# Second experts: each slot tile's weights fetched by SyncE into a ring, against weights resident in SBUF and addressed by register

## The reference

```python
logits = x_flat @ Wr + br
probs = jax.nn.softmax(logits, axis=-1)
topk_w, topk_idx = jax.lax.top_k(probs, 2)              # of 16 experts
topk_w = topk_w / jnp.clip(jnp.sum(topk_w, axis=-1, keepdims=True), 1e-09)
h = jnp.einsum('nc,ech->neh', x_flat, W1) + b1
h = jax.nn.gelu(_layernorm(h, g1, be1), approximate=False)
expert_out = jnp.einsum('neh,eho->neo', h, W2) + b2
sel = jnp.take_along_axis(expert_out, topk_idx[:, :, None], axis=1)
y_flat = jnp.sum(sel * topk_w[:, :, None], axis=1)
```

## Time and profile before

| | before |
|---|---|
| median of 3 runs | 3978.86 us (3962.93 to 3979.88) |
| profiled execution | 3980.16 us, its span 3977.9 |
| mean granted TensorE clock | 0.877 |
| busy share of the span: TensorE, VectorE, ScalarE, GpSimd | 70%, 61%, 40%, 47% |
| second experts | 3439.8 (first load) to about 3787 us of the span |
| two attentions | 2323 to about 3190 us |

### The profile page before, as it was taken

One profiled execution on the slowest core, in us unless ns is written; L12 is line 12 of the kernel. 1 busy time (PEld: TensorE's weight loads), 2 busy tenths in 40 slices (PEclk: granted clock), 3 DMA queues, 4 the chain that ended last, 5 costly groups with the idle time before them and its releaser, 6 DMA issues.

```text
span 3977.9 us, 93960 instructions
## 1 busy us (share of the span) xinstructions
PE 2801.2 (70%) x28526; PEld 1944.6 (49%) x28529; DVE 2445.7 (61%) x6828; ACT 1588.0 (40%) x3994; POOL 1863.6 (47%) x2306
## 2 busy tenths in 40 slices
PE   3999999758888888882058879999999930266600
PEld 2666666435555555551036656666666620255500
DVE  2777777528878878884001148888888860155545
ACT  2666666424545545541013335555555510011100
POOL 4222222006766666663730036666666617411177
PEclk9999999978989989985579989999999965699955
DMA  2111111351111111111222211111111102211133
GB/s 52 42 41 39 39 41 44 117 172 42 50 47 49 48 48 49 47 32 34 77 71 74 67 39 30 30 28 30 29 30 30 26 11 78 64 55 55 54 85 87
DMA packets 282379, 207.17 MB, mean 52 GB/s; under 512 B 61731, under 2 KB 246456, under 8 KB 281905
## 3 DMA queue, kind: packets, MB, share of 16 engines
q1 hardware_dynamic: 262960, 164.88, 14.1%
q0 software_dynamic: 19200, 39.62, 3.7%
HBM read 114.99 MB, written 90.18 MB: 52 GB/s over the span
## 4 chain that ended last, share of the span: by engine, by line
issue 21%; PE 14%; POOL 13%; DVE 5%; POOLq 0%; ACT 0%; DMA 0%; DVEq 0%; ACTq 0%; SPq 0%
PE scores_ps L1049 3%; POOL k_bd L2001 2%; POOL rows L2053 2%; POOL shared L2152 2%; POOL shared L2001 2%; POOL got L2098 2%; PE heads_ps L1056 1%; PE desk_ps L1056 1%; PE scores_ps L1167 1%; POOL norm_rstd L1997 1%; PE scores_ps L1169 1%; PE heads_ps L1167 1%; DVE e_T L1821 1%; PE desk_ps L1167 1%; POOL rstd L2160 1%
## 5 line engine op out<-in xcount | busy, mean ns | idle before, releaser
L1997 POOL TENSOR_TENSOR norm_rstd<-norm_veps,minus_half 128x1 f32<-128x1 f32 x384 | 218.3, 569 | 380.6 <-DVE norm_veps L1557 374.8
L2053 POOL DMA_INDIRECT rows<-e_in,slot_put x256 | 248.9, 972 | 164.0 <-issue 107.4
L1278 ACT ACTIVATE probs<-probs 128x512 f32<-128x512 f32 x384 | 239.9, 625 | 107.6 <-DVE probs L1577 107.2
L1575 DVE TENSOR_REDUCE row_max<-scores_ps 128x8 f32<-128x512 f32 x384 | 261.9, 682 | 26.0 <-issue 16.1
L1577 DVE TENSOR_TENSOR probs<-scores_ps,row_max 128x512 f32<-128x512 f32 x384 | 265.4, 691 | 13.2
L1282 ACT ACTIVATE turned<-scores_ps 128x512 f32<-128x512 f32 x384 | 228.1, 594 | 109.2 <-PE scores_ps L907 103.5
L907 PE MATMUL scores_ps<-consts,probs 128*128 128x128 f32 x1536 | 243.1, 282 | 7.3 <-ACT probs L1278 6.5
L1210 ACT ACTIVATE probs<-probs 128x512 f32<-128x512 f32 x256 | 161.4, 630 | 141.4 <-DVE probs L1496 138.5
L1494 DVE TENSOR_REDUCE row_max<-scores_ps 128x8 f32<-128x512 f32 x256 | 174.7, 682 | 57.0 <-PE scores_ps L763 57.0
L2142 POOL TENSOR_TENSOR o_rstd<-o_veps,minus_half 128x2 f32<-128x2 f32 x72 | 49.9, 693 | 288.7 <-DVE o_veps L1926 288.7
L907 PEld LDWEIGHTS scores_ps<-consts,probs 128*128 128x128 f32 x1536 | 176.2, 143 | 16.0 <-ACT probs L1278 9.8
(11 more groups left out here) (335 smaller groups left out, 8327.6 us busy)
## 6 DMA issues: line engine op xcount, KB each, us to landing
hop_dram<-shared SPq DMA_DIRECT2D x64, 256.0 KB, 2.1
hop_in<-hop_dram SPq DMA_DIRECT2D x64, 256.0 KB, 3.0
rows<-zero_rows SPq DMA_DIRECT2D x64, 144.0 KB, 1.9
shared<-rows SPq DMA_DIRECT2D x72, 128.0 KB, 2.1
moe<-shared SPq DMA_DIRECT2D x72, 128.0 KB, 1.8
rows<-zero_rows SPq DMA_DIRECT2D x64, 128.0 KB, 1.8
c_in<-in_ctx SPq DMA_DIRECT2D x128, 64.0 KB, 1.9
c_two<-in_ctx SPq DMA_DIRECT2D x128, 64.0 KB, 2.4
```

What stands on the lines that cost most here:

```text
L1278: act.activation(half, half, ACT.Exp, scale=scale).then_inc(at.exped.sem, 1)
L1575: dve.tensor_reduce(best, sc, AX, ALU.max).then_inc(at.shift.sem, 1)
L1997: pool.tensor_tensor(n_rstd[:, k, u, :], n_veps[:, k, u, :], minus_half[:, 0:1], ALU.pow).then_inc(sig.sem, 1)
L2053: pool.indirect_dma_start(out=rows, out_offset=bass.IndirectOffsetOnAxis(ap=slot_put[:, c, U * n + i:U * n + i + 1], axis=0), in_=put_rows ...
```

## The change

The second mixture's weights no longer stay in SBUF. At the start of the third stage they are written to a packed table in DRAM, `e_dram`: 128 rows of 258 numbers per expert, W1, W2, scale and shift side by side. In the sixth stage SyncE reads the pair's two expert numbers and copies two experts' 128 x 258 numbers (132 KB each) into a ring of four places, `fetched`, one place a pair; a place is written when the second layer of the pair four before is done. TensorE and ScalarE take weights, scale and shift from the place at fixed addresses, and wait for its two transfers. The biases lie in 16 rows, `bias_rows`; the bias matmul now has as its stationary input a one-hot column of the expert (`chosen`), which GpSimd copies for each pair out of a table, `expert_row`, that one new VectorE instruction in the second routing makes. In `combine5` the copy is gone: the two multiply-adds read their weights from the table by a register, and the counts of `norms[0]` fall from 7 to 6 a tile. GpSimd also clears `bias_rows` at the start, for which SyncE's first waits count one more.

```diff
--- before.py
+++ after.py
@@ -172,8 +172,9 @@
         hop_rows = sb("hop_rows", [P, HOPS, D])
         hop_T = sb("hop_T", [P, HOPS, P])
-        o_w1, o_w2 = hop_rows[:, 0:E1, :], hop_rows[:, E1:2 * E1, :]
-        o_b1, o_b2 = hop_T[:, 0:E1, :], hop_T[:, E1:2 * E1, :]
+        EW = 2 * P + 2
+        fetched, chosen = sb("fetched", [P, V, 2, EW]), sb("chosen", [P, V, 2])
+        bias_rows = sb("bias_rows", [P, 2 * P])
...
+        e_dram = dram("e_dram", [E1 * P, EW])
+        e_rows = e_dram.rearrange("(e p) n -> e p n", p=P)
...
@@ -438,11 +440,10 @@
-            (o_w1, T["L1_ffn_W1"].rearrange("e c h -> c e h")),
-            (o_w2, T["L1_ffn_W2"].rearrange("e c h -> c e h")),
-            (o_b1.rearrange("p e h -> p (e h)"), T["L1_ffn_b1"].rearrange("e h -> (e h)").partition_broadcast(P)),
-            (o_b2.rearrange("p e h -> p (e h)"), T["L1_ffn_b2"].rearrange("e h -> (e h)").partition_broadcast(P)),
-            (o_g[:], T["L1_ffn_g1"].rearrange("e h -> h e")), (o_b[:], T["L1_ffn_be1"].rearrange("e h -> h e")),
+            (e_rows[:, :, 0:P], T["L1_ffn_W1"]), (e_rows[:, :, P:2 * P], T["L1_ffn_W2"]),
+            (e_rows[:, :, 2 * P:2 * P + 1], T["L1_ffn_g1"].rearrange("e (h o) -> e h o", o=1)),
+            (e_rows[:, :, 2 * P + 1:EW], T["L1_ffn_be1"].rearrange("e (h o) -> e h o", o=1)),
+            (bias_rows[0:E1, 0:P], T["L1_ffn_b1"]), (bias_rows[0:E1, P:2 * P], T["L1_ffn_b2"]),
...
+            def fetch(q, k):
+                experts = [sp.value_load(expert_of[0:1, bass.ds(2 * q + i, 1)], min_val=0, max_val=E1 - 1) for i in range(2)]
+                after(sp, (s["o_down"], q - 1))
+                for i, e in enumerate(experts):
+                    sp.dma_start(fetched[:, k, i, :], e_rows[bass.ds(e, 1)].rearrange("e p n -> p (e n)"))\
+                      .then_inc(e_fetched[k], 16)
+
+            sp.wait_ge(late, 16 * len(late_loads))
+            sp.wait_ge(routed, 2)
+
             def period(i, j, live_pair):
                 w = j % 2
                 if live_pair(i + 3):
                     load6(i + 3, 1 - w)
+                    fetch(i + 3, (j + 3) % V)
                 if live_pair(i - 2):
                     store6(i - 2, w)
...
-            def layer(q, w, bank, src, weights, biases, waits, done):
-
-                experts = experts_of(q)
-                after(pe, *waits)
-                for i, e in enumerate(experts):
-                    pe.matmul(bank[:, cols(i)], const("row0"), biases[:, bass.ds(e, 1), :].rearrange("p e h -> p (e h)"),
+            def layer(n, q, k, bank, src, waits, done):
+
+                after(pe, (e_chosen, q + 1), (e_fetched[k], 8 * (q - k) + 32), *waits)
+                part = slice(P * n, P * n + P)
+                for i in range(2):
+                    pe.matmul(bank[:, cols(i)], chosen[:, k, i:i + 1].broadcast_to([P, P]), bias_rows[:, part],
                               start=True, stop=False, skip_group_check=True)
-                    last = pe.matmul(bank[:, cols(i)], src[:, cols(i)],
-                                     weights[:, bass.ds(e, 1), :].rearrange("p e h -> p (e h)"),
+                    last = pe.matmul(bank[:, cols(i)], src[:, cols(i)], fetched[:, k, i, part],
                                      start=False, stop=True, skip_group_check=True)
                 last.then_inc(done, 1)
...
@@ -1432,13 +1440,11 @@
-                    experts = [act.value_load(expert_of[0:1, bass.ds(2 * i + k, 1)], min_val=0, max_val=E1 - 1)
-                               for k in range(2)]
-                    after(act, (s["o_down"], i + 1), (s["o_hturned"], i + 3))
-                    for k, e in enumerate(experts):
+                    after(act, (e_fetched[j], 8 * (i - j) + 32), (s["o_down"], i + 1), (s["o_hturned"], i + 3))
+                    for k in range(2):
                         cols = slice(P * k, P * k + P)
                         last = act.activation(o_g_T[w][:, cols], scores_ps[:, w, 1, cols], ACT.Gelu,
-                                              scale=o_g[:, bass.ds(e, 1)], bias=o_b[:, bass.ds(e, 1)])
+                                              scale=fetched[:, j, k, 2 * P:2 * P + 1], bias=fetched[:, j, k, 2 * P + 1:EW])
...
+                    link(dve.tensor_scalar(expert_row[:], r_ej[:], float(E - 1), const("lane"), ALU.min, ALU.is_equal))
...
             def combine5(n, u):
-                dve.tensor_copy(got_w[u], weight[:, :, bass.ds(n, 1)].rearrange("p k t -> p (k t)")).then_inc(norms[0].sem, 1)
-                after(dve, norms[0].of(n, 1), (in_loaded[u], X4_LOADS + 8 * (n - u) + 16), (got_loaded[u], 16 * (n - u) + 32))
-                dve.scalar_tensor_tensor(part_sum[u], got[u][:, 0:D], got_w[u][:, 0:1], x_in[u], ALU.mult, ALU.add)\
+                after(dve, (in_loaded[u], X4_LOADS + 8 * (n - u) + 16), (got_loaded[u], 16 * (n - u) + 32))
+                dve.scalar_tensor_tensor(part_sum[u], got[u][:, 0:D], weight[:, 0, bass.ds(n, 1)], x_in[u], ALU.mult, ALU.add)\
                    .then_inc(norms[0].sem, 1)
-                after(dve, norms[0].of(n, 2))
-                dve.scalar_tensor_tensor(x4_raw[u], got[u][:, D:2 * D], got_w[u][:, 1:2], part_sum[u], ALU.mult, ALU.add)\
+                after(dve, norms[0].of(n, 1))
+                dve.scalar_tensor_tensor(x4_raw[u], got[u][:, D:2 * D], weight[:, 1, bass.ds(n, 1)], part_sum[u], ALU.mult, ALU.add)\
                    .then_inc(norms[0].sem, 1)
...
+                if live_pair(i + 2):
+                    after(pool, (s["o_down"], i + 1))
+                    pool.tensor_copy(chosen[:, (j + 2) % V, :], expert_row[:, bass.ds(2 * (i + 2), 2)]).then_inc(e_chosen, 1)
                 if live_pair(i + 1):
                     pool.wait_ge(s["o_veps_done"], i + 4)
```

More of the change, by code:

```diff
@@ L83, in constants @@
     f["head8q"] = f["head4"] * MD ** -0.5
-    f["row0"] = (p[:, None] == 0) & (p[None, :] >= 0)
+    f["lane"] = p[:, None]
     b = {"tri16": p[:, None] <= p[None, :], "ones16": np.ones((P, P)), "ident16": np.eye(P), "causal16": np.where(t[None, :] <= (p % S)[:, None], 0.0, NEG)}
@@ L224, in build @@
         assert NJ % (2 * V) == 0
-        expert_of = sb("expert_of", [P, NJ], I32)
+        expert_of, expert_row = sb("expert_of", [P, NJ], I32), sb("expert_row", [P, NJ])
         slot_f, weight = sb("slot_f", [P, 2, NT]), sb("weight", [P, 2, NT])
@@ L261, in build @@
         logits1 = sb("logits1", [P, NT, E1])
-        o_g, o_b = sb("o_g", [P, E1]), sb("o_b", [P, E1])
         o_in, o_in_T, o_hn, o_g_T, o_out = (views(U * 2 * P * k, 2 * P) for k in range(5))
@@ L310, in build @@
         o_in_loaded, o_stored = ([sem(f"{k}{u}") for u in range(U)] for k in ("o_in_loaded", "o_stored"))
+        e_fetched, e_chosen = [sem(f"expert_weights_fetched{k}") for k in range(V)], sem("expert_chosen")
         z_loaded, z_stored = hx_loaded, x_stored
@@ L389, in build @@
         o_copied = [Signal(pad_copied, NT), Signal(oT_copied, NT)]
-        norms = [again(mixed, 7), again(m_shift, 4), again(f_norm, 4)]
+        norms = [again(mixed, 6), again(m_shift, 4), again(f_norm, 4)]
         norm_rstd = [again(m_rstd), again(f_rstd), again(r4_added)]
@@ L515, in _ @@
                 load1(n, n)
-            sp.wait_ge(zero_sem, 1)
+            sp.wait_ge(zero_sem, 2)
             def clear(n):
@@ L650, in load_x4 @@
             def load_x4(n, u):
-                after(sp, norms[0].of(n - 2, 2))
+                after(sp, norms[0].of(n - 2, 1))
                 sp.dma_start(x_in[u], tile_rows(r4_dram, n)).then_inc(in_loaded[u], 16)
@@ L1148, in _ @@
             pe.wait_ge(counts_read, 2)
-            def experts_of(q):
-                return [pe.value_load(expert_of[0:1, bass.ds(2 * q + i, 1)], min_val=0, max_val=E1 - 1) for i in range(2)]
             def cols(i):
@@ L1176, in period @@
                 if live_pair(i + 1):
-                    layer(i + 1, 1 - w, scores_ps[:, 1 - w, 0, :], o_in_T[1 - w], o_w1, o_b1,
+                    layer(0, i + 1, (j + 1) % V, scores_ps[:, 1 - w, 0, :], o_in_T[1 - w],
                           ((s["o_T_done"], i + 4), (s["o_hn_done"], i + 2)), s["o_up"])
@@ L1186, in period @@
                 if live_pair(i - 1):
-                    layer(i - 1, 1 - w, (heads_ps, desk_ps)[1 - w], o_g_T[1 - w], o_w2, o_b2,
+                    layer(1, i - 1, (j - 1) % V, (heads_ps, desk_ps)[1 - w], o_g_T[1 - w],
                           ((s["o_g_done"], i + 2), (s["o_out_done"], i)), s["o_down"])
@@ L1867, in period @@
                     combine5(i + 3, 1 - u)
-                    stats5(norms[0], 3, 0, i + 3, 1 - u, x4_raw[1 - u])
+                    stats5(norms[0], 2, 0, i + 3, 1 - u, x4_raw[1 - u])
                 if live(i):
@@ L1954, in _ @@
             pool.memset(zero_rows[:], 0.0).then_inc(zero_sem, 1)
+            pool.memset(bias_rows[:], 0.0).then_inc(zero_sem, 1)
             pool.memset(slot_get[:], 0)
@@ L2092, in get5 @@
             def get5(n, u):
-                after(pool, norms[0].of(n - 2, 3))
```

(1 more changed line is left out.)

## The result

The changed kernel took 3906.1 us in the median (four runs, 3896.88 to 3922.08), the kernel before 3979.24 in the runs beside it: a ratio of 0.9842, 95% interval 0.9818 to 0.9866. That is 1.6% faster, 73 us, and 4 us from the forecast. The execution that was profiled is the slowest of the four: 3922.08 us, its span 3919.9 and so 58 us shorter than the one of before. What is known of the 16 us by which it stands above its median is told at the end.

What follows compares the result with a forecast made beforehand. No engine bounds the whole; the second experts are bound by TensorE's register reads, in series with a chain through the engines. Terms: -61 + 2 - 8 - 3 = -70 us from the profiled 3980.16, giving 3910 us, range 3880 to 3935.

Steps and rivals of the forecast that it cites:

- SyncE becomes the bound: Second experts: SyncE's serial list of load, two reads, two fetches and store sets the period, 3.7 us a pair.
- 3.0 as TensorE's floor: Second experts: TensorE's own work, 216 / 72 = 3.0 us a pair, as the least period.
- two to three pairs ahead: Second experts: a fetch goes out 7 to 11 us before its use and lands in 2 to 3 us.
- The saving of 61 us: Second experts: period from 4.62 to 3.7 us, 0.92 us saved a pair, times 66 pairs.
- The combination, 8 us: Attentions: without the weight copy, the multiply-add takes over its wait for GpSimd; 8 us saved, between 0 and 33.
- The weights' load: Start of third stage: two 1 MB broadcasts dropped, packing into DRAM added; -3 us taken, between -9 and +7.
- the bytes do leave: Start of third stage: half of the load's bytes dropped, pieces as many as before; a reason for taking -3 us.
- The bound of +7: Start of third stage: if the small pieces cost twice as much, 7.4 us more.
- (1): Second experts: SyncE keeps up and TensorE's 3.0 us bounds; saving 107 us, total 3865; chance 0.16.
- (2): Second experts: SyncE's reads cost 0.56 us, not 0.28; period 4.26, saving 24 us, total 3947; chance 0.13.
- (3): Second experts: a computed-address fetch costs its issuer 1.4 us; period 5.3, 46 us slower, total 4017; chance 0.04.
- (4): Second experts: fetch not ahead, TensorE waits for each landing, one wait replaces another; about 3970; chance 0.05.

Runs made afterwards that it cites:

- the split run: Changed kernel with store on ScalarE's queue, table's loads moved to the first scatter, ScalarE also reading the second expert number and issuing its fetch: 3822.61 us (0.9613).

## Why the prediction was right, point by point

- **SyncE becomes the bound: right.** Forecast 3.7 us a pair, measured 3.86. Taking the store out of its list took 0.67 us off the period, reading the numbers twice put 1.08 on, and moving half of the list away uncovered the next bound at 2.99. The prediction had 3.0 as TensorE's floor, and that agreement is luck: the floor was the busy time of before divided by 72, but in the split run the same matmuls are busy for 2.54 us a pair, and the bound is the round through TensorE and VectorE. One step on the way was wrong too: that a fetch is "two to three pairs ahead" and its wait "met early in the steady part". In the change the first layer starts 2.3 us after its second fetch is issued (median), 63 of the 72 first layers wait for their fetch, and the lead of the ring is used up by SyncE's lateness. That TensorE's register reads were the bound before is read from the earlier trace rows and from the "issue" that went away; no run took the reads alone out.
- **The saving of 61 us: the number right, its parts not.** The period of before was mis-sized: the prediction took a pair of the transposes' records for missing, but all 144 are in the trace, so the 305 us hold 65 pairs and not 66, 4.69 us and not 4.62; the loads' own row gives 4.70. With 3.86 for 3.7 the loop saved 63 x (4.70 - 3.86) = 53 us, and not 61. The rest came where no term stood: at the end, from the loop's last load to the last store's issue, 26.4 us before (3758.1 to 3784.5) became 15.8 (3710.6 to 3726.4). Those are 11 us; a likely reason is that the last pairs have hardly any reads and fetches left to wait for. The start cost 2.3 more (22.1 to 24.4 us from the first load to the loop), forecast 2. That the sum of it is 61 again is luck.

```profile
L688 SPq DMA_DIRECT2D moe<-shared x72: 372/390/397, 3456.3 to 3784.5; - x72
```

- **The combination, 8 us: right, 9 measured**, and by the mechanism: the multiply-add takes 1.85 us in the median, the wait passed on. The Trainium skill, "SBUF — State Buffer", section "Who interferes with whom", has it that a VectorE instruction with two SBUF inputs contends with a GpSimd one that reads SBUF, that a copy can, and that on this chip a reduction never does. The traces agree: 1.85 us for the multiply-add, 1.73 for the copy, 0.146 for the reduction. The saving per tile was overrated, 0.17 us and not 0.3 (2.43 us from the end of the instruction in front to the end of the second multiply-add, against 2.26); 0.10 of the difference is the register step between the two multiply-adds. TensorE's gap before the transpose fell by 5.6 us in 52 tiles, 6.9 in 64; what the other 2 us are isn't shown.
- **The weights' load: wrong.** Forecast -3 us, measured +4.2. The step that failed is "the bytes do leave", as a reason for a gain. 2 MB did leave, and SyncE stands no shorter: 6.41 and 4.86 us in the columns and 3.75 in the small biases, where the last column alone took 7.42 before. Taking the small pieces away gave 5.8 us, and taking all six loads away 17.7; so the wait goes with the transfers that stayed, small pieces and matrices, and not with the bytes that left. The bound of +7 held.
- **Rivals.** (1) SyncE doesn't keep up; (2) its reads take 0.27 us, and the 600 ns of the Trainium skill, "DMA: Bandwidth & Descriptors", section "Latency and other measured facts", are not what this trace shows; (3) a fetch costs 0.35 us, not 1.4; (4) TensorE does wait for fetches, but for late ones: before the first layer the wait is 55.9 us in the change, 26.7 with the store moved, 77.3 with the reads doubled and 2.8 in the split, so it follows the length of SyncE's list and isn't the way round the ring.
- **The sum.** -61 - 9 + 4 = -66 by the three stages, where -70 was forecast; the medians say -73, the profiled executions -58. Of the 8 us between -66 and -58, 4.5 are the third stage (876.8 us before and 881.3 after from the first to the last load of `hop_in`), and 2.8 lie between the combination's last load and the first pair's, 297.9 and 300.7 us; in the other runs with the same routing this takes 297.5 to 300.0, so it is scatter.

## What to carry to other kernels

An instruction stream that is taken off one engine lands on another, and its sum there is a period as well: add up what the receiving list does per turn, register steps and transfer issues included, before calling the engine idle because its busy time is small. Here each 0.1 us in SyncE's list was worth some 6 us of the kernel, and moving one transfer to another engine's queue gave 43 us in the stage on top of the change. A wait that ends with another engine's instruction isn't removed with the instruction that shows it; look for a row in which the first one slipped through, and see who waited then.

## What was not expected of the hardware

- A whole run of one kernel scatters by some 25 us, and most of it seems to be the third stage's: from the first to the last load of `hop_in` the profiles of before, of the change and of its nine edits lie between 861 and 885 us. Its code is the same in the changed kernel and in the run with the store moved, yet it took 881 us in one and 863 in the other, at granted clocks of 0.90 and 0.92 over the stage (columns as in the section on the result):

```profile
890.00:1790.00 900.00, 749.61 (x7253) 500.25 (x7252) 729.68 (x2366) 442.27 (x1154) 575.95 (x732) 0.90 0.16 46
```

```profile
890.00:1790.00 900.00, 742.61 (x7403) 495.79 (x7403) 749.48 (x2426) 450.58 (x1179) 587.36 (x749) 0.92 0.16 46
```

The first experts, the attentions and the second experts repeat to within 3 us where nothing was changed in them. This fits the 16 us by which the changed kernel's profiled execution lies above its median, though its other executions have no profile, and it is why stages, not medians, settle the small questions here. What makes the clock differ between executions of the same code was not tried.
- A reduction over one element moves two numbers in 0.146 us where a copy of the same two numbers waits 1.7 us for GpSimd.
